# Delta-rule scan: products without a use of their result in every second step of steps 4 to 19, instead of in each

## The reference

```
def body(S, inp):
    q_i, k_i, u_i, w_i = inp
    attn = jnp.where(tri, jnp.einsum('bhcd,bhed->bhce', q_i, k_i), 0.0)
    u_i = u_i - w_i @ S
    o_i = q_i @ S + attn @ u_i
    S = S + jnp.einsum('bhcd,bhce->bhde', k_i, u_i)
    return (S, o_i)
S, o = jax.lax.scan(body, S0, (mv(qc), mv(kc), mv(u), mv(w)))
```

## Time and profile before

| | us |
|---|---|
| median of 3 runs | 585.35 (583.8 to 586.37) |
| the profiled execution | 584.6 |
| its span, as the profile's times run | 582.8 |
| scan, step 1 to step 30, in the span's times | about 481.7 to 514.8 |
| steps 4 to 19 | 486.68 to 504.37 |

### The profile page before, as it was taken

One profiled execution on the slowest core, in us unless ns is written; L12 is line 12 of the kernel. 1 busy time (PEld: TensorE's weight loads), 2 busy tenths in 40 slices (PEclk: granted clock), 3 DMA queues, 4 the chain that ended last, 5 costly groups with the idle time before them and its releaser, 6 DMA issues.

```text
span 582.8 us, 17528 instructions
## 1 busy us (share of the span) xinstructions
PE 546.2 (94%) x7486; PEld 372.8 (64%) x7486; DVE 395.0 (68%) x766; ACT 325.5 (56%) x575; POOL 177.9 (31%) x343
## 2 busy tenths in 40 slices
PE   3799999999999999999999999999999789989995
PEld 2445555555555556777778777776676577667774
DVE  5697999999999945345362534445789951479685
ACT  2327888788888876656656554656913330135441
POOL 7100111453554433001010102548986325010202
PEclk9799999999999999999999999999999889999998
DMA  4868756555432000001000000022294300000001
GB/s 122 178 203 209 211 131 154 104 125 97 74 58 58 3 4 2 0 1 38 1 1 1 1 1 0 5 52 39 54 133 95 74 4 3 5 3 1 0 20 54
DMA packets 54227, 33.82 MB, mean 58 GB/s; under 512 B 39029, under 2 KB 45685, under 8 KB 54150
## 3 DMA queue, kind: packets, MB, share of 16 engines
q1 hardware_dynamic: 48998, 31.65, 24.5%
q10 hardware_dynamic: 5152, 1.05, 1.1%
HBM read 20.83 MB, written 9.44 MB: 52 GB/s over the span
## 4 chain that ended last, share of the span: by engine, by line
PE 76%; DVE 12%; ACT 5%; DMA 4%; issue 2%; SPq 1%; POOL 0%; POOLq 0%; DVEq 0%; ACTq 0%
PE ps L1843 11%; PE ps L1828 10%; PE ps L1590 7%; PE ps L1592 7%; PE ps L1591 7%; PE ps L2031 3%; DVE inv_flat L549 3%; PE ps L1807 3%; PE ps L2163 3%; PE ps L2164 3%; DVE inv_flat L551 2%; ACT prob L703 2%; DMA qst<-shift_sb 2%; PE ps L2023 2%; PE ps L1680 2%
## 5 line engine op out<-in xcount | busy, mean ns | idle before, releaser
L1246 DVE TENSOR_REDUCE nmx<-ps 128x1 f32<-128x1024 f32 x128 | 154.0, 1217 | 14.7 <-PE ps L1808 13.4
L703 ACT ACTIVATE prob<-ps 128x512 f32<-128x512 f32 x256 | 137.4, 597 | 26.3 <-PE ps L1828 25.8
L1843 PE MATMUL ps<-prob,vp 128*32 128x128 f32 x2048 | 78.9, 278 | 0.0
L1828 PE MATMUL ps<-qst,kst 50*128 50x512 f32 x256 | 73.5, 491 | 4.4 <-ACT prob L703 3.5
L1843 PEld LDWEIGHTS ps<-prob,vp 128*32 128x32 f32 x2048 | 49.1, 109 | 39.8 <-ACT prob L703 22.4
L1118 DVE TENSOR_TENSOR h_lo<-hf,h_hi 128x512 fp32r<-128x512 f32 x48 | 33.1, 689 | 52.4 <-ACT h_hi L607 50.2
L1590 PE MATMUL ps<-h_hi,w_lo 128*128 128x512 f32 x144 | 58.2, 404 | 2.4 <-DVE h_lo L1118 2.4
L1592 PE MATMUL ps<-h_hi,w_hi 128*128 128x512 f32 x144 | 56.9, 395 | 0.0
L1591 PE MATMUL ps<-h_lo,w_hi 128*128 128x512 f32 x144 | 56.8, 394 | 0.0
L1807 PE MATMUL ps<-kst,qst 48*128 48x512 f32 x128 | 52.6, 412 | 0.6 <-DVE nmx L1246 0.5
L1808 PE MATMUL ps<-kst,qst 48*128 48x512 f32 x128 | 51.5, 404 | 0.0
(11 more groups left out here) (262 smaller groups left out, 1094.6 us busy)
## 6 DMA issues: line engine op xcount, KB each, us to landing
qst<-q_scratch SPq DMA_DIRECT2D x31, 192.0 KB, 4.5
kst<-k_scratch SPq DMA_DIRECT2D x31, 192.0 KB, 4.9
w_raw<-L_ffn_h_w SPq DMA_DIRECT2D x8, 256.0 KB, 3.7
kd<-ka SPq DMA_DIRECT2D x8, 256.0 KB, 6.4
X<-L_attn_x SPq DMA_DIRECT2D x4, 256.0 KB, 5.3
qst<-shift_sb SPq DMA_DIRECT2D x64, 4.0 KB
q_scratch<-w_hi SPq DMA_DIRECT2D x2, 512.0 KB, 5.1
k_scratch<-w_lo SPq DMA_DIRECT2D x2, 512.0 KB, 3.0
```

The source lines that it names most:

```text
L703: nc.scalar.activation(prob[:, n % PROBS, GT * (t % 2):GT * (t % 2) + GT], ps[:, RINGB + i % RING, :], ACT.Exp, scale=SCORE_SCALE).then_in ...
L1246: nc.vector.tensor_reduce(nmx[:, u % 2, j:j + 1], pair, AX.X, ALU.max, negate=True).then_inc(max_done, 1)
L1828: nc.tensor.matmul(ps[:, RINGB + i % RING, :], kst[r:r + 50, p, P * t:P * t + P], half_of(qst[r:r + 50, p, :], u % 2), start=True, stop=Tr ...
L1843: last = nc.tensor.matmul(ps[32 * j:32 * j + 32, PVB, P * half:P * half + P], vp[:, h, t, :], prob[:, n % PROBS, c:c + P], start=(t == 0), ...
```

## The change

In steps 4 to 19 the product without a use stays in the even steps and is taken out of the odd ones (5, 7, ... 19): eight products, that is eight weight loads and eight matmuls. Steps 1 to 3 keep two, steps 20 to 27 keep one each. No wait and no semaphore is touched.

```diff
-                if j < 28:
-                    keep_busy((j + 1) % 2, 2 if j < 4 else 1)
+                if j < 4:
+                    keep_busy((j + 1) % 2, 2)
+                elif j < 28 and (j % 2 == 0 or j >= 20):
+                    keep_busy((j + 1) % 2, 1)
```

## The result

The changed kernel takes 591.13 us in the median (589.57 to 592.69, 4 runs) against 584.68 us before (583.80 to 586.37, 4 runs): the ratio is 1.0104, with a 95% interval of 1.0074 to 1.0133. It is slower, by some 6 us. Measured again beside other kernels it was 590.13 us against 584.46 us, ratio 1.0080 (1.0054 to 1.0107). The profiled execution took 589.65 us.

The account below looks back on a forecast made before the run. TensorE's own order bounds steps 4 to 19, with instruction blocks as second bound. Slack 1.03 + 0.04 = 1.07 us plus 0.13 us for the shorter program gives 1.2 us: 585.35 - 1.2 = 584.15 us, range 581.8 to 586.5 us.

Parts of the forecast that it names:

- The bound: Steps 4 to 19: TensorE's own order bounds the 1.09 us step; the filler has 0.43 us on the path.
- the 0.68 us of the prediction: Length of an odd step without its filler, against 1.09 us now, if nothing else bound.
- The instruction blocks take back most of the 3.2 us: Steps 4 to 19: blocks of 256 instructions, about 3.45 us apart, cut the upper end of 3.2 us to 1.2 us.
- the slack of 1.03 us: Four packet distances from 488.45 to 503.28 took 14.83 us, against 13.80 us at 3.45 us each.
- a pause behind step 30: The pause at 516.10, where the gain was to be 1.07 us, plus 0.13 us for the shorter program.
- The clock: Thinned steps 4 to 19: TensorE works 1.75 of 2.18 us a pair of steps, 80%, so the clock should hold.
- the second window: 510.88 to 514.29, steps 27 to 30 before the change: TensorE busy 3.12 us, clock still 1.00.
- The factor of 1.75: Slowdown at half clock, from fillers at 0.40 us against 0.23 us, applied to whole steps.
- the clock rival: Steps 5 to 20: the clock falls in the thinned steps; +3.5 us net, 588.9 us, chance 0.16.
- Nothing arrives: The slack before the block borders isn't usable: only -0.2 us, 585.1 us, chance 0.14.
- all of it arrives: Steps 4 to 19: the blocks' pace is no bound or blocks lie in stock; -3.2 us, 582.1 us, chance 0.14.

Follow-up runs that it names:

- the shifted kernel: The kernel before with 64 more pairs of weight load and product, half a block, where TensorE waits ahead of the scan: 586.49 us in one run.

## Why the prediction was wrong

**The bound.** Right. TensorE's own order was the bound of steps 4 to 19, and the odd steps became as long as worked out. VectorE's additions in the kernel after are one step apart:

```profile
488.47 0.23 DVE L1495 TENSOR_TENSOR state<-ps,prep 128x64 f32<-128x64 f32 x1 [0.94 <-PE ps L2097]
489.15 0.23 DVE L1495 TENSOR_TENSOR state<-ps,prep 128x64 f32<-128x64 f32 x1 [0.45 <-PE ps L2097]
490.25 0.23 DVE L1495 TENSOR_TENSOR state<-ps,prep 128x64 f32<-128x64 f32 x1 [0.88 <-PE ps L2097]
...
500.24 0.23 DVE L1495 TENSOR_TENSOR state<-ps,prep 128x64 f32<-128x64 f32 x1 [0.94 <-PE ps L2097]
502.06 0.23 DVE L1495 TENSOR_TENSOR state<-ps,prep 128x64 f32<-128x64 f32 x1 [1.60 <-PE ps L2097]
```

From 488.47 to 489.15 are the 0.68 us of the prediction, and 489.15 to 490.25 is a step with a filler, 1.10 us. The last two, 1.82 us apart, have a pause between them.

**The instruction blocks take back most of the 3.2 us.** Right in kind, and in part luck in size. New pauses stand inside runs of products in the kernel after, 3.45 to 3.7 us apart:

```profile
491.09 0.14 PEld L2065 LDWEIGHTS ps<-state,kq 32*32 32x32 f32 x4 [0.23 <-issue]
...
494.54 0.30 PEld L2023 LDWEIGHTS ps<-inv_flat,kd 64*64 64x64 f32 x6 [0.22 <-issue]
...
498.00 0.17 PEld L2097 LDWEIGHTS ps<-state,tT 32*32 32x32 f32 x9 [0.41 <-issue]
...
501.72 0.14 PEld L2097 LDWEIGHTS ps<-state,tT 32*32 32x32 f32 x6 [1.06 <-issue]
```

491.09, 494.54 and 498.00 are 3.45 us apart, as predicted, and 501.72 is 3.72 us behind the last. So 3.45 us is the least distance, not the constant that my sum made of it; that one block cost 0.27 us of the slack of 1.03 us. The measured gain of steps 4 to 19 is 0.90 us, a little of it already eaten by the last 0.7 us at half clock. The forecast was 1.2 us at a pause behind step 30, where the lost clock leaves nothing to compare, so the size is borne out only as far as step 19; that the pauses sit at block borders is borne out by the shifted kernel. The 3.45 us themselves are the pace of some executions: in the profile without the fillers of 5, 7 and 9 the blocks came 3.73 us apart, and there the same sum would have found no slack. The rule of the Trainium skill, "Runtime: NRT & Kernel Launch", section "Instruction fetch mechanics", that a border is mostly hidden, doesn't hold for the tiny products of this scan: pauses of 0.2 to 1.1 us stand at its borders in the kernel after.

**The clock: the step that failed.** Of the 2.18 us of a pair of steps the prediction says: "In it TensorE works for about 1.09 + 0.66 = 1.75 us, 80%, far nearer to the second window than to the first. I expect the clock to hold." It gave the fall a chance of 0.16. So the sum had nothing for a lost clock, and the time came out some 7 us over the forecast: 1.2 us less were forecast, and some 6 us more were measured. The busy share was the wrong measure. It came out higher than the 80%, 14.85 of 16.12 us or 92% up to the fall, and the clock fell nevertheless. With 100% busy and 256 columns it fell in four of four executions. In one profile of the changed kernel the window before the fall was busy for 2.46 of 3.41 us, in the other for 3.05 of 3.40 us. The windows of the earlier trace rows that I compared differ in busy share, but the one that held, 510.88 to 514.29, also had wide products in it (a filler, transposes and projections of 128 by 128), and I let the modelled busy time of 32 by 32 products count as much as theirs. Had I asked which products kept the clock, and not how long TensorE was occupied, the groups of the earlier trace rows would have pointed at the answer: the only 128 by 128 products in steps 4 to 19 are the fillers, and the change halves them. The prediction has this very argument in favour of the rival and let the 80% outweigh it. That the fillers' amount is the cause is what the experiments show: with the amount given back in the even steps alone, eight of ten executions kept the clock, and with half of it evenly spread none did.

**The price of the rival.** It was put at +3.5 us net for 13.65 us at half clock, 0.29 us for each. Its step lengths were too long: 1.71 and 0.99 us at half clock against the 1.9 and 1.16 us of the prediction, a mean of 1.35 us and not 1.53 us, so by the same sum 0.19 us for each us at half clock. The factor of 1.75 was taken from fillers alone, and these ran partly at full clock (3.23 us from 460.66 on, and the clock is 1.00 from 463.09); whole steps stretched by 1.57 and 1.46 only (1.71 against 1.09 us, 0.99 against 0.68 us). What was missing on the other side is how long the low clock lasts. The prediction had named steps 20 to 27 slow as well, at 5 to 6 us in all, but priced the rival without them, as if these steps, which held the clock before with one filler each, would give it back. They hold a full clock and in no profile raise a low one, not even with two fillers each. So the stretch was 20.5 us in one profile and 34.1 us in the other, and the 3.30 us of steps 20 to 27 is the largest single loss, in steps that the change doesn't touch. The measured +6 us is the clock rival with that addition; the 588.9 us were too low by 1 to 2 us.

**Nothing arrives, and all of it arrives.** Neither: 0.90 us came in steps 4 to 19.

## What to carry to other kernels

Products that only hold the clock must be judged by the clock, not by their own cost: taking half of them out was slower here than keeping all and than having none, as the clock goes and the rest is still paid, at 0.72 us each and not 0.41 us. Test both ends, all and none; here none was as fast as all (584.28 against 584.47 us beside it), as the small products lose little at half clock and the fillers' own time is gone. In a stretch of tiny products count instructions as well as work: in this scan TensorE paused for the next block where 256 instructions were worked off in less than 3.45 to 3.75 us, and a product taken out there gives little.

## What the runs showed of the hardware

- Holding the full clock and regaining it are different things. Steps 20 to 27 with one filler each held it through 7.42 us; at half clock the same steps didn't regain it in 10.72 us, nor with two fillers in 13.75 us. It came back behind the last state, among 128 by 128 products (fillers, transposes and projections), between 518 and 529 us in the profiles.
- A TensorE that the profile shows busy for 3.40 of 3.40 us can lose its clock: it did with fillers of 256 columns among 32 by 32 and 64 by 64 products.
- The kernel before stands near that edge itself: 5 of 76 executions lost the clock. The same program keeps it in one execution and loses it in another, and the runs don't show what decides.
- Small products lose little at half clock: steps 20 to 27 without fillers took 7.93 us, against 7.42 us at full clock with fillers.
- Blocks of 256 TensorE instructions, where TensorE waited for them, came 3.45 us apart at the least and 3.7 us in some cases. By the strips of the DMA rate a packet moves 2.3 to 2.9 us before the pause at its border ends (488.75 to 491.09 in the kernel after, 490.90 to 493.52 without the fillers of 5, 7 and 9), and the next one 1.0 to 1.1 us after that end (492.15 and 494.65). It is the first of the two that varies; why, wasn't found.
- Left open: whether uneven spacing makes a loss more likely at the same amount. 3 of 20 against 5 of 76 doesn't tell.
